# Attention output kept token-major in a cross-attention and mixture kernel, with three engine queues re-ordered

## What is computed

```
# attention: 32 heads of 8, 64 queries and 64 keys per sequence
q = rope((layernorm(x) @ Wq).reshape(b, n, 32, 8), pos)
k, v = split(ctx @ Wkv);  k = rope(k, pos)
w = softmax(einsum('bqhd,bkhd->bhqk', q, k) / sqrt(8), axis=-1)
attn = einsum('bhqk,bkhd->bqhd', w, v).reshape(b, n, 256)
x = x + attn @ Wout + bout
# soft mixture: 16 experts, 128 slots each, hidden 64
x_ln = layernorm(layernorm(x)) * gamma + beta
logits = einsum('bnd,des->bnes', l2norm(x_ln) * scale, l2norm(mu))
slot_in = einsum('bnd,bnes->besd', x_ln, softmax(logits, axis=1))
h = gelu(einsum('besd,edh->besh', slot_in, W1) + b1)
out = x + einsum('bsd,bns->bnd', (h @ W2 + b2), softmax(logits over e and s))
```

## Time and profile before

| | us |
|---|---|
| median of 3 runs | 526.37 |
| lowest and highest | 526.05, 526.86 |
| the profiled execution's own time | 526.87 |
| its span in the trace | 525.0 |
| PE, DVE, ACT, POOL busy | 471.5, 373.4, 300.5, 146.4 |

### The profile page before, as it was taken

One profiled execution on the slowest core, in us unless ns is written; L12 is line 12 of the kernel. 1 busy time (PEld: TensorE's weight loads), 2 busy tenths in 40 slices (PEclk: granted clock), 3 DMA queues, 4 the chain that ended last, 5 costly groups with the idle time before them and its releaser, 6 DMA issues.

```text
span 525.0 us, 14893 instructions
## 1 busy us (share of the span) xinstructions
PE 471.5 (90%) x5776; PEld 378.8 (72%) x5776; DVE 373.4 (71%) x861; ACT 300.5 (57%) x595; POOL 146.4 (28%) x247
## 2 busy tenths in 40 slices
PE   0768899898888888969999999999999999999995
PEld 0545666666556564758888888888888888988884
DVE  5688989888889989475666575657657565755653
ACT  1345665556666555608447745854774585468454
POOL 3409511238393903211311211221121112112100
PEclk9969999999999999989999999999999999999999
DMA  6600000073001200000000000000000000000000
GB/s 184 227 7 6 7 7 6 8 165 90 7 10 36 32 0 2 2 1 1 12 11 2 12 11 0 10 10 10 0 10 10 7 3 10 10 0 10 11 12 10
DMA packets 16018, 12.75 MB, mean 24 GB/s; under 512 B 7232, under 2 KB 15344, under 8 KB 15600
## 3 DMA queue, kind: packets, MB, share of 16 engines
q1 hardware_dynamic: 15984, 12.27, 8.1%
HBM read 10.16 MB, written 2.11 MB: 23 GB/s over the span
## 4 chain that ended last, share of the span: by engine, by line
PE 60%; DVE 24%; ACT 8%; issue 5%; SPq 1%; DMA 1%; DVEq 1%; POOL 0%; ACTq 0%
PE psum L938 14%; PE psum L939 12%; PE psum L940 12%; PE psum L1149 9%; PE psum L1164 6%; DVE mx L689 5%; DVE rc L706 4%; DVE pb L694 3%; ACT vb L494 3%; PE psum L1017 2%; DVE pb L853 2%; DVE xT_l L658 2%; DVE ra L665 1%; DVE qkr L676 1%; ACT mu_raw L556 1%
## 5 line engine op out<-in xcount | busy, mean ns | idle before, releaser
L556 ACT COPY mu_raw<-psum 128x384 f32<-128x384 f32 x96 | 41.0, 445 | 116.4 <-PE psum L1149 116.4
L831 DVE TENSOR_REDUCE es<-eb 128x4 f32<-128x512 f32 x64 | 42.9, 686 | 61.2 <-ACT eb L548 61.1
L477 ACT ACTIVATE pb<-pb 128x512 f32<-128x512 f32 x64 | 39.3, 631 | 75.0 <-DVE pb L694 75.0
L1149 PE MATMUL psum<-w_raw,eb 64*128 64x129 f32 x1024 | 68.8, 286 | 3.0 <-DVE w_raw L824 1.9
L1149 PEld LDWEIGHTS psum<-w_raw,eb 64*128 64x128 f32 x1024 | 62.8, 193 | 8.2 <-DVE pb L853 4.0
L348 POOL TENSOR_TENSOR sm<-sm,mhalf 128x1 f32<-128x1 f32 x16 | 8.8, 551 | 169.9 <-DVE sm L810 169.9
L938 PE MATMUL psum<-mun_h,xlT_l 128*128 128x512 f32 x128 | 52.2, 408 | 0.2 <-DVE xlT_l L817 0.2
L1003 PE MATMUL psum<-ident,pb 128*128 128x128 f32 x256 | 42.2, 290 | 10.8 <-ACT vb L494 8.8
L853 DVE TENSOR_TENSOR pb<-psum,rh 128x384 f32<-128x384 f32 x96 | 49.3, 514 | 3.3
L1003 PEld LDWEIGHTS psum<-ident,pb 128*128 128x128 f32 x256 | 28.2, 145 | 31.5 <-issue 24.1
L940 PE MATMUL psum<-mun_h,xlT_h 128*128 128x512 f32 x128 | 50.6, 395 | 0.0
(11 more groups left out here) (156 smaller groups left out, 1076.6 us busy)
## 6 DMA issues: line engine op xcount, KB each, us to landing
mu_raw<-in_L_ffn_mu SPq DMA_DIRECT2D x1, 2048.0 KB, 12.9
out<-w_raw SPq DMA_DIRECT2D x16, 128.0 KB, 1.7
xa<-in_x SPq DMA_DIRECT2D x1, 1536.0 KB, 8.5
ctile<-in_ctx SPq DMA_DIRECT2D x16, 64.0 KB, 1.8
eb<-mur_scratch SPq DMA_DIRECT2D x1, 1024.0 KB, 4.9
w_raw<-in_L_ffn_W SPq DMA_DIRECT2D x2, 512.0 KB, 7.9
w_raw<-in_L_ffn_W SPq DMA_DIRECT2D x1, 1024.0 KB, 9.3
xa<-in_x SPq DMA_DIRECT2D x1, 512.0 KB, 3.5
```

Source lines behind the costliest of these rows:

```text
L556: a.copy(eT[:, e0:e0 + n, :].rearrange("p n (b k) -> p b n k", b=2), pair(i, n)[:, :, :, HC:XC]).then_inc(eT_ready, 1)
L831: v.reduce_sum(es[:, 4 * c:4 * c + 4], eb[:, 4 * c:4 * c + 4, :], AX.X).then_inc(es_ready, 1)
L1149: m = mm(bank[HB[i % 3] + b][:, n * XC:(n + 1) * XC], eb[rows, e, :], xw[rows, e, :], start=True, stop=True)
```

## The change

- `attend` becomes token-major: `pT` is the stationary operand (64 columns, one sequence), and `vb` streams. `vb` now holds, for each pair of heads q, 18 columns: 8 values of the one head, 8 of the other (each in its half of the partitions) and 2 columns of ones. So one matmul gives both heads' outputs and both sums: 32 matmuls of 18 columns in place of 48 of 64 or 128 columns. `hone` and its matmuls are gone.
- `normalise` takes the reciprocal of 128x32 sums and multiplies 128x256 by it with a broadcast, into a new tile `on`.
- New: `transpose_o` (PE, two transposes of `on` into bank 5) and `oT_copy` (ACT, bank 5 to `oT`).
- ACT copies three groups of `pT`, then `oT`, then the fourth group, and runs all four exponentials behind that.
- DVE normalises ahead of `xT_low`; the clamp of the mu norms moves behind the residual, and PE's wait for it from `project_out` to `transpose_o` of step 7; `mu_sums` moves ahead of `project_qk`.
- The end of the stage is re-ordered on PE, DVE and ACT.

```
@@ attend
-                for half in range(2):
-                    for b in range(2):
-                        for r in range(2):
-                            for g in range(GROUPS):
-                                c = 256 * r + 32 * (half * GROUPS + g)
-                                product(half, r, g, vb[:, p, b].rearrange("p r c -> p (r c)")[:, c:c + 32],
-                                        slice(64 * b, 64 * b + 64), half * P + b * 64)
-                    for r in range(2):
-                        for g in range(GROUPS):
-                            m = product(half, r, g, hone[:, r, :], slice(0, P), DIM + half * P)
+                for q in range(HEADS // 2):
+                    i = 4 * (q % 8 // 2) + 2 * (q // 8) + q % 2
+                    for b in range(2):
+                        rows = slice(64 * b, 64 * b + 64)
+                        m = mm(bank[4][rows, q * VC:(q + 1) * VC], pT[:, i, rows], vb[:, p, b, q, :],
+                               start=True, stop=True)
                 m.then_inc(o_filled, 1)
+
+            def transpose_o(t, clamped=False):
+                pe.wait_ge(on_ready, t + 1)
+                wait(pe, x1_ready, t)
+                if clamped:
+                    pe.wait_ge(muss_clamped, 1)
+                for k in range(KD):
+                    m = nc.tensor.transpose(bank[5][:, k * P:(k + 1) * P], on[:, k * P:(k + 1) * P], ident[:])
+                m.then_inc(oT_filled, 1)
...
@@ normalise
-                v.reciprocal(rc[:], bank[4][:, DIM:2 * DIM]).then_inc(rc_done, 1)
+                src = bank[4][:, 0:HEADS // 2 * VC].rearrange("p (q c) -> p q c", c=VC)
+                v.reciprocal(rc[:].rearrange("p (q j) -> p q j", j=2), src[:, :, 2 * HD:VC]).then_inc(rc_done, 1)
                 dve.wait_ge(rc_done, t + 1)
-                v.tensor_tensor(oT[:], bank[4][:, 0:DIM], rc[:], ALU.mult).then_inc(oT_ready, 1)
+                wait(dve, oT_filled, t)
+                v.tensor_tensor(on[:].rearrange("p (q j d) -> p q j d", j=2, d=HD),
+                                src[:, :, 0:2 * HD].rearrange("p q (j d) -> p q j d", j=2),
...
@@ DVE step
+                if before:
+                    normalise(s - 1)
                 if ahead:
                     xT_low(s + 2)
-                if before:
-                    normalise(s - 1)
...
@@ ACT step
-                for g0 in (0, 2):
-                    if before:
-                        for gr in (g0, g0 + 1):
-                            pT_copy(s - 1, gr)
-                    for gr in (g0, g0 + 1):
-                        exp_group(s, p, gr)
+                if before:
+                    for gr in range(3):
+                        pT_copy(s - 1, gr)
+                    if out:
+                        oT_copy(s - 2)
+                    pT_copy(s - 1, 3)
+                for gr in range(GROUPS):
+                    exp_group(s, p, gr)
...
@@ DVE, end of the stage
-            xlT_copy(0)
             clamp(0, 0)
+            xlT_copy(0)
             normalise(TILES - 2)
-            residual(TILES - 2)
...
+            slot_sums(0, range(2))
+            residual(TILES - 2)
+            slot_sums(0, range(2, 4))
+            normalise(TILES - 1)
             dve.wait_ge(xw_const, 3)
-            slot_sums(0)
-            sums(0, 0)
-            normalise(TILES - 1)
-            residual(TILES - 1)
             xw_copy(0)
             xlT_copy(1)
+            residual(TILES - 1)
+            dve.wait_ge(es_zeroed, 1)
+            sums(0, 0)
             ffn_step(0, 0)
```

More of the change, by code:

```diff
@@ L36 @@
 XC = HC + SEQ
+VC = 2 * HD + 2
 def wait(eng, sem, value):
@@ L508, in xT_high, with oT_copy, step @@
                 a.copy(flat(xT[0]), bank[7][:, 0:3 * P]).then_inc(xT_split, 1)
-            def step(s, p, before=True, after=True, ahead=True):
-                for g0 in (0, 2):
-                    if before:
-                        for gr in (g0, g0 + 1):
-                            pT_copy(s - 1, gr)
-                    for gr in (g0, g0 + 1):
-                        exp_group(s, p, gr)
+            def oT_copy(t):
+                act.wait_ge(oT_filled, t + 1)
+                wait(act, a_filled, t)
+                a.copy(oT[:], bank[5][:, 0:DIM]).then_inc(oT_ready, 1)
+            def step(s, p, before=True, after=True, out=True, ahead=True):
+                if before:
[6 more added lines that the diff above has]
+                    exp_group(s, p, gr)
                 if after:
@@ L531, in _ @@
             step(0, 0, before=False)
-            step(1, 1)
+            step(1, 1, out=False)
             with act.Fori(1, TILES // 2 - 1) as i:
@@ L583, in _ @@
                 pT_copy(TILES - 1, gr)
-            slot_exps(0, 0)
+            sumsq(1, 1)
+            slot_exps(0, 0, range(2))
+            oT_copy(TILES - 2)
             for gr in range(2, 4):
                 pT_copy(TILES - 1, gr)
-            sumsq(1, 1)
+            slot_exps(0, 0, range(2, 4))
+            oT_copy(TILES - 1)
             with act.Fori(0, TILES // 2 - 1) as i:
@@ L722, in step @@
                     rope_sums(s + 1)
+                softmax(s, p, 2)
+                if out:
+                    residual(s - 2)
                 if norms:
@@ L825, in xw_copy, with slot_sums @@
                                     b1b[:, 8 * c:8 * c + 8, :], ALU.add).then_inc(xw_ready, 1)
-            def slot_sums(t):
-                for c in range(4):
+            def slot_sums(t, chunks=range(4)):
+                for c in chunks:
                     dve.wait_ge(e_ready, t * 4 + c + 1)
@@ L1050, in mu_sums, with step @@
                     m.then_inc(muss_ready, 1)
-            def step(s, p, before=True, after=True, out=True, ahead=True, norms=None):
+            def step(s, p, before=True, after=True, out=True, ahead=True, norms=None, clamped=False):
                 if before:
@@ L1063, in step @@
                     transpose_p(s - 1, 1 - p, 2)
+                if norms is not None:
+                    mu_sums(s, norms)
+                if out:
+                    transpose_o(s - 2, clamped)
                 if after and before:
@@ L1066, in step @@
                 logits(s, 2, 0)
-                if norms is not None:
-                    mu_sums(s, norms)
                 if before:
@@ L1109, in transpose_xl, with slot_logits @@
                 m.then_inc(xlT_filled, 1)
-            def slot_logits(t):
+            def slot_logits(t, chunks=range(4)):
                 pe.wait_ge(xlT_ready, t + 1)
-                for c in range(4):
+                for c in chunks:
                     if c == 2:
```

62 lines of the change are left out of this document (27 added, 35 removed).

## The result

| | before | changed |
|---|---|---|
| median, same chip | 526.62 us, 6 runs | 515.58 us, 6 runs |
| lowest and highest | 526.05, 530.59 | 511.32, 519.52 |
| ratio (95% interval) | | 0.973 (0.966 to 0.980) |
| the profiled execution and its span | 526.87, 525.0 | 519.52, 517.6 |
| PE, DVE, ACT, POOL busy | 471.5, 373.4, 300.5, 146.4 | 476.5, 351.6, 305.7, 146.0 |

The ratio and its interval leave out two of the six runs, 519.52 and 519.29 us, which were counted as slow ones; the medians of all six give 0.979.

A forecast was written before the change was run, and what follows sets the result against it. Attention steps were taken as bound by a DVE loop, then by near-equal ACT and PE loops. Steps 6.9, end of stage 4.0 and clock 2.1 sum to 13.0 us off 526.87: 513.9 profiled, 513.4 median, range 507.5 to 522.

The forecast's parts named there:

- Of the 2.1 us only 0.7 come through: Attention step: DVE alone would save 2.1 us, but logits come later, so the step only shortens to 11.32 us.
- ACT loop: Attention step: maximum, residual, value copies, key copies on ACT, next logits, next maximum; claimed 11.32 us a step.
- Rival 2: Attention steps: logits are ready earlier, so DVE's own 9.5 us sets the step; 487 us in all, chance 0.05.
- Rival 4: `attend`: weight loads don't overlap, 61 ns each, `attend` 3.9 us, 13.3 us a step; 543.7 us, slower; chance 0.08.
- The PE loop: Attention step: logits, transposes, projections, `attend`, value copies, back to logits; claimed about 11.3 us, with no slack left.
- These four steps come to 11.35 + 0.9: Steps 3 to 6: `mu_sums` ahead of the projections adds 0.9 us, making 12.25 us a step; gain 0.2 us together.
- Rival 1: Attention steps: PE's queue takes their gain, with 0.6 us more for waits or `attend`; 521.4 us, chance 0.11.
- rival 3: Whole kernel: no change in effect, within 0.2%; the end gives its 4 us back to a wait for ACT; chance 0.04.
- Steps 13 and 14: Late attention steps: DVE's slack hides the small moments in step 13, gain 1.75 us; step 14 gains nothing.
- The end of the stage: From `expand(0)` to the first dispatch: normalisation done during `expand` removes PE's waits; gain 4.0 us.
- Without waits of 2.3 and 2.0 us the clock should stay: First dispatch: the clock stays at 2.4 GHz, 4.22 us instead of 6.33; gain 2.1 us, lost if it falls.
- Dispatch about 11 us earlier than 233.43: Sign for the forecast: the first dispatch after the attention stage starts about 11 us earlier and takes 4.2 us.

The follow-up runs named there:

- recip_only: The kernel before with only the reciprocal and its use cut to 32 of 256 columns, output not the reference's: 518.59 us, ratio 0.981.
- attend_half: The changed kernel with every second `attend` matmul only, each streaming 36 columns, output not the reference's: 524.7 us in one execution.
- max_half: The changed kernel with the maximum taken over the first 32 of a head's 64 keys: 506.04 us in one run.
- attend_wide: The changed kernel with 54 columns instead of 18 streamed in each `attend` matmul, the surplus overwritten: 512.06 us, ratio 0.971 to before.
- norm_late: The changed kernel with `normalise` behind the low part of the split (`xT_low`), as before: 519.29 us.
- end_old: The changed kernel with before's order at the end of the stage on PE, DVE and ACT: 522.81 us.
- again: The changed kernel run once more, unedited: 518.65 us over six runs, ratio 0.982 to before.

## Why the prediction was right, and where not

**The reciprocal and the product.** 0.35 and 0.42, as worked out from the rows of other widths.

**"Of the 2.1 us only 0.7 come through."** Right, and by the mechanism that was forecast: 11.32 to 11.34 a step, forecast 11.32 from the ACT loop and 11.35 taken. `recip_only` shows that it is the reciprocal that gives it. That the loop through DVE and ACT binds is shown by `attend_half`, whose step stays, and `max_half`, whose step falls. DVE's wait is 1.42, forecast 1.3. Rival 2, DVE's pace, fails by this wait.

**`attend`.** 1.95 us from the nearest row, 1.95 measured. Whether load or stream sets it was left open; `attend_wide` and `attend_half` show that it is the load. Rival 4, loads that pass singly, fails with it (its sum was 0.8 us short as well: by its own terms steps 13 and 14 lose 2.3 us, not 1.7, and the four with `mu_sums` 7.6, not 7.4). The rule in the Trainium skill, "TensorE: Matmul & The Clock Gate", LDWEIGHTS and Part 3, would have made it an estimated 3.4 us or more. The trace disagrees, with 30 ns a record and all rows used.

**The PE loop was mis-sized.** I had 11.26 and said that it and the ACT loop come out equal. `max_half` measures 10.95. In the pieces: the six transposes, 0.59 + 0.38 in my sum, take 109.31 - 108.68 = 0.63; the two new ones add 0.14 behind the four, as they need no gap of their own. Projections to `attend` take 4.40, not 4.55; `attend` to the copies 2.15 in `max_half`, not 2.04. Together, with 0.03 more from there to the logits, 0.35 less. For steps 7 to 12 it made no difference. For `mu_sums` it did: "These four steps come to 11.35 + 0.9" took the slack as nil, and the 0.9 us meet 0.37 of slack first: 11.83, not 12.25, and a gain of 1.84 us instead of 0.2. `max_half` bears this out, with 11.83 in those steps and 10.95 in the others. Rival 1 rests on the same mistake, and the gain rules out rival 3.

**Steps 13 and 14** came out at 1.76 and 0, as forecast (the latter in `attend_wide`'s trace); `norm_late` shows that 0.4 of the former is the move ahead of the split.

**The end of the stage.** 3.8 us of the forecast 4.0 from `expand(0)` on, 3.99 from step 15's first maximum where the clock doesn't fall. 1.41 of it is the reciprocal's (`recip_only`).

**The clock.** "Without waits of 2.3 and 2.0 us the clock should stay": at the dispatch it did, 2.1 us. The reason given isn't shown: `end_old` kept its clock there with waits of 1.00, 0.46 and 1.95 us, and `recip_only` lost it with 0.94 and 1.95. And "kept or lost" was asked for this one place. That an edit could make it fall elsewhere was in neither the forecast nor a rival, though the same edit cut `attend`'s streamed columns from 64 and 128 to 18. It costs 7.0 us in 12 of 16 runs. So the sign "Dispatch about 11 us earlier than 233.43" failed in the profiled execution, with 5.3; in `attend_wide`'s, without the fall, it is 13.2.

**The sum.** Without the fall: 8.7 for the steps, 4.0 and 2.1, 14.8 us; 526.87 - 14.8 = 512.1, and those runs lie at 511.2 to 512.4. With it 519.1, and they lie at 518.3 to 520.3. That the forecast of 513.4 lies 2.2 us from the median of 515.58 is luck: one term was 1.6 too small and another, 7 us in most runs, was missing, and the first six runs fell three and three. In `again` the median is 518.65. The range held every run.

**What stays open:** why a run falls or not, with the same program on the same chip; what besides the narrow stream it takes; the two groups of before (2 to 4 us apart, the upper with a lower mean clock, and only the lower seen in a trace); and the two later runs of `attend_wide`.

## What to carry to other kernels

Write each step as a set of loops, one for each engine that carries it, and price them piece by piece: a gain on one engine ends at the next loop, and work put on another is free up to that loop's slack, which shortening the binding engine in an experiment measures directly. Here the layout was worth its trouble for the vector instruction that it shortened, not for the matmuls that it saved. When work moves to a later step, follow everything that is queued behind it on the other engines, the DMA queue included. Look at the granted clock over the whole program after every edit that thins out TensorE's streams, and over several runs; if it falls, a useless matmul in each step can be cheaper than the fall.

## What the runs showed of the hardware

- The granted clock fell to 1.2 GHz for 17 us, at 197.8 us, after a stretch in which PE was busy 9.43 of 10 us. The kernel before, at the same place of its step 14, had PE busy for less, 3.13 of 5 us, as its row below shows, waited 1.04 us as well, and kept 2.4 GHz. So neither the busy time nor the wait foretold the fall. With 54 columns instead of 18 in `attend`, or one more matmul in the step, no run lay in the upper group.
- A reciprocal of 256 fp32 columns took 1748 ns and one of 32 columns 0.35 us, on the line that the rows of 6 and 2 columns gave (148 ns and 6.25 ns a column, an estimate from rows 4 and 5). A product of 256 columns takes 0.42 us.

The kernel before, busy time from 200 to 205 us, columns as above; PE's is the first after the length, the clock is the 1.00:

```profile
200.00:205.00 5.00, 3.13 (x103) 2.54 (x103) 4.86 (x11) 2.66 (x8) 0.15 (x1) 1.00 0.02 3
```
